# An LSTM and a conditioned adapter on one core: seeds of the first two steps in transfers of their own, the projection's weights on ScalarE's queue, five more zero matmuls

## The reference

```python
B, T, D = 16, 256, 256;  H = 256;  RANK = 8
xz = einsum('ntd,dk->ntk', x, Wx) + b              # the projection, 4 gates x 256
def step((h, c), xz_t):                            # 256 steps, one behind the other
    i, f, o, g = split(xz_t + h @ Wh)
    c = sigmoid(f) * c + sigmoid(i) * tanh(g)
    h = sigmoid(o) * tanh(c)
x = x + scan(step, (cond, 0), xz)

cn = layernorm(cond) * gamma + beta
a1, b1, a2, b2 = split(gelu(cn @ W1 + bias1) @ W2 + bias2)     # each (B, 256, 8)
mid = gelu(x @ base_down + (x @ a2) @ b2.T)
out = x + mid @ base_up.T + a1 @ (b1 . mid)
```

## Time and profile before

| | |
|---|---|
| median of 3 runs | 622.96 us (622.89, 622.96, 625.73) |
| the profiled execution | 622.3 us, span 620.3 us |
| granted TensorE clock, mean | 0.994 |
| TensorE busy | 600.6 us, 97% of the span |
| VectorE busy | 478.7 us, 77% |
| ScalarE busy | 386.7 us, 62% |
| GpSimd busy | 38.2 us, 6% |
| step 0's first matmul | 21.01 us into the span |
| step 1's first matmul | 25.18 us |

### The profile page before, as it was taken

One profiled execution on the slowest core, in us unless ns is written; L12 is line 12 of the kernel. 1 busy time (PEld: TensorE's weight loads), 2 busy tenths in 40 slices (PEclk: granted clock), 3 DMA queues, 4 the chain that ended last, 5 costly groups with the idle time before them and its releaser, 6 DMA issues.

```text
span 620.3 us, 34579 instructions
## 1 busy us (share of the span) xinstructions
PE 600.6 (97%) x14176; PEld 441.2 (71%) x14176; DVE 478.7 (77%) x2548; ACT 386.7 (62%) x2158; POOL 38.2 (6%) x78
## 2 busy tenths in 40 slices
PE   8789999999999999999999999999999999999997
PEld 5565555777777777777777777777777777777886
DVE  3566666888888888888888888888888888888773
ACT  2365555666666666666666666666666666666662
POOL 3000000000000000000000000000000000000000
PEclk9799999999999999999999999999999999999999
DMA  5893530232222113232321232322023232321201
GB/s 159 231 218 142 180 45 12 38 46 54 55 54 39 35 39 54 55 54 54 54 36 25 53 54 54 54 54 45 26 43 54 55 54 54 54 37 21 47 20 35
DMA packets 31471, 38.74 MB, mean 62 GB/s; under 512 B 3601, under 2 KB 29505, under 8 KB 30290
## 3 DMA queue, kind: packets, MB, share of 16 engines
q1 hardware_dynamic: 31282, 36.51, 27.4%
q0 software_dynamic: 32, 0.03, 0.0%
HBM read 15.55 MB, written 4.19 MB: 32 GB/s over the span
## 4 chain that ended last, share of the span: by engine, by line
PE 85%; DVE 7%; POOL 4%; issue 2%; DMA 1%; SPq 0%; POOLq 0%; ACT 0%; DVEq 0%; ACTq 0%
PE z L674 32%; PE x_bank L496 17%; PE aux L522 8%; PE z_o L674 7%; PE out_bank L545 5%; PE out_bank L603 4%; POOL xp L934 4%; PE aux L507 3%; PE aux L474 2%; PE out_bank L553 2%; PE aux L529 2%; DVE z L821 2%; DVE prod L831 1%; DVE gates L836 1%; DVE h_t L843 1%
## 5 line engine op out<-in xcount | busy, mean ns | idle before, releaser
L674 PEld LDWEIGHTS z<-wh,h_t 128*16 128x16 f32 x8160 | 155.1, 96 | 119.6 <-DVE h_t L843 96.0
L674 PE MATMUL z<-wh,h_t 128*16 128x96 f32 x8160 | 228.1, 248 | 5.6 <-DVE h_t L843 2.3
L821 DVE STREAM_TRANSPOSE z<-z 128x96 f32<-128x96 f32 x512 | 151.5, 298 | 87.2 <-PE z L674 60.3
L412 ACT ACTIVATE gates<-z 128x48 f32<-128x48 f32 x512 | 107.7, 210 | 141.9 <-DVE z L821 114.3
L496 PE MATMUL x_bank<-wx,x_t 128*128 128x256 f32 x512 | 156.2, 393 | 0.5 <-ACT x_t L330 0.5
L336 ACT ACTIVATE z<-seed 128x96 f32<-128x96 f32 x512 | 123.7, 242 | 5.6 <-DMA seed<-proj 5.6
L674 PE MATMUL z_o<-wh,h_t 128*16 128x64 f32 x4080 | 105.7, 219 | 0.4
L831 DVE SCALAR_TENSOR_TENSOR prod<-gates 128x32 f32<-128x32 f32 x512 | 97.8, 191 | 0.6
L836 DVE SCALAR_TENSOR_TENSOR gates<-prod 128x16 f32<-128x16 f32 x512 | 84.3, 165 | 8.7
L496 PEld LDWEIGHTS x_bank<-wx,x_t 128*128 128x128 f32 x512 | 80.7, 195 | 6.4 <-issue 1.5
L674 PEld LDWEIGHTS z_o<-wh,h_t 128*16 128x16 f32 x4080 | 80.6, 97 | 1.2 <-issue 0.9
(11 more groups left out here) (109 smaller groups left out, 445.9 us busy)
## 6 DMA issues: line engine op xcount, KB each, us to landing
seed<-proj SPq DMA_DIRECT2D x128, 128.0 KB, 4.0
w<-in_L_cond_W SPq DMA_DIRECT2D x4, 2048.0 KB, 9.9
x_nat<-in_x SPq DMA_DIRECT2D x32, 128.0 KB, 4.0
out<-y_nat SPq DMA_DIRECT2D x32, 128.0 KB, 3.7
wx<-in_L_cond_Wx SPq DMA_DIRECT2D x2, 512.0 KB, 5.6
wh<-in_L_cond_Wh SPq DMA_DIRECT2D x2, 256.0 KB, 6.5
wh<-in_L_cond_Wh SPq DMA_DIRECT2D x1, 512.0 KB, 6.2
w<-in_L_cond_W SPq DMA_DIRECT2D x1, 256.0 KB, 4.3
```

The source lines that it names most:

```text
L412: act.activation(gates[s % 2][m][:, 0:3 * B].rearrange("p (g b) -> p g b", b=B), zt[m].rearrange("p (g c) -> p g c", c=C)[:, :, 0:B], ACT. ...
L674: ins = pe.matmul(dst, h_prev[:, kc, :], rhs, start=False, stop=(kc == 1), skip_group_check=True)
L821: dve.transpose(zt[m], z_bank[m][:, 0:GC]).then_inc(turned[m], 1)
```

## The change

- A new tile `first_seed` holds the seeds of steps 0 and 1 (FIRST = 2). It is filled by eight transfers of 16 KB, four a step: SyncE issues those of quadrants 0 and 1, ScalarE those of quadrants 2 and 3, each in the order step 0, step 1, after the last quarter is in `proj`. Each step has its own semaphore. GpSimd clears `first_seed` ahead of the two `seed` tiles.
- The four full transfers of block 0 stay, with all eight steps in them, and are issued by SyncE behind its four small ones. ScalarE waits for them at the end of step 0 instead of ahead of it; steps 0 and 1 read `first_seed`, steps from 2 on `seed`.
- ScalarE issues the two transfers of Wx as its first instructions, ahead of its table load. SyncE's next loads move up by two.
- On ScalarE the doubling of Wh's g columns comes ahead of the copy of x of block 1 instead of behind it.
- TensorE runs five zero matmuls (128x96, into a projection bank) between the bias products and the projection.

```diff
+WARM_TILES = 5
+FIRST = 2
...
+        first_seed = sb("first_seed", [P, FIRST, ZW])
...
+        first_loaded = [sem(f"first_loaded{t}") for t in range(FIRST)]
...
+        def load_first_seeds(engine, quadrants):
+
+            engine.wait_ge(seeds_zeroed, 1)
+            engine.wait_ge(xz_ready, XQ)
+            for t in range(FIRST):
+                for j in quadrants:
+                    engine.dma_start(first_seed[32 * j:32 * j + B, t, :], proj[0][t:P:TB, ZW * j:ZW * (j + 1)])\
+                          .then_inc(first_loaded[t], 16)
...
     @block.sync: load_seed
-                    sp.wait_ge(seeds_zeroed, f.k + 1)
+                    sp.wait_ge(seeds_zeroed, f.k + 2)
...
-            load_cols(wx, Wx, 0, 0, 2 * H, "wx_if")
-            load_cols(wx, Wx, 2 * H, 2 * H, 2 * H, "wx_og")
...
+            load_first_seeds(sp, (0, 1))
             load_seed(Blk(0, 0))
             load_x(Blk(0, 0, 2))
...
     @block.scalar
+            load_cols(act, wx, Wx, 0, 0, 2 * H, "wx_if")
+            load_cols(act, wx, Wx, 2 * H, 2 * H, 2 * H, "wx_og")
             act.wait_ge(zeroed, 1)
...
-            evacuate_x(Blk(0, 1))
             act.wait_ge(w_loaded["wh"], 48)
             double_g(wh, 2 * H, wh_ready)
+            evacuate_x(Blk(0, 1))
+            load_first_seeds(act, (2, 3))
             act.wait_ge(bits_set, 1)
-            act.wait_ge(seed_loaded[0], 16 * NQ)
+            act.wait_ge(first_loaded[0], 16 * NQ)
             for m in both:
-                seed_bank(0, 0, m)
-            seed_o(0, 0)
+                seed_bank(first_seed, 0, m)
+            seed_o(first_seed, 0)
+            act.wait_ge(first_loaded[1], 16 * NQ)
...
+                    source = seed[ahead.par] if ahead.at_least(1) or s_next >= FIRST else first_seed
...
+                    if s == FIRST - 2 and not k.at_least(1):
+                        act.wait_ge(seed_loaded[0], 16 * NQ)
...
     @block.tensor
+            for i in range(WARM_TILES):
+                pe.matmul(x_bank[0][:, 0:GC], zeros[:, :], zeros[:, 0:GC], start=True, stop=True)
             project(Blk(0, 0), range(N_PIECES))
...
     @block.gpsimd
+            pool.memset(first_seed[:, :, :], 0.0).then_inc(seeds_zeroed, 1)
```

More of the change, by code:

```diff
@@ L231, in lstm_adapter, with load_cols @@
         last, last_early = follower(end), early(end)
+        def load_first_seeds(engine, quadrants):
[5 more added lines that the diff above has]
+                          .then_inc(first_loaded[t], 16)
+        by_half = "(m p) n -> p m n"
+        def load_cols(engine, dst, src, lo, src_lo, n, name):
+            engine.dma_start(dst[:, :, lo:lo + n], src.rearrange(by_half, m=NM)[:, :, src_lo:src_lo + n])\
+                  .then_inc(w_loaded[name], 16)
         @block.sync
@@ L258, in store_y @@
                   .then_inc(stored[a.lane][a.seq.par], 16)
[L260 to L264, removed]
             w2_q = W2.rearrange("(k p) (q n) -> q p k n", p=P, q=4)
@@ L272, in _ @@
             sp.dma_start(b_row[:, :], b.rearrange("(a n) -> a n", a=1)).then_inc(w_loaded["b"], 16)
-            load_cols(wx, Wx, 0, 0, 2 * H, "wx_if")
-            load_cols(wx, Wx, 2 * H, 2 * H, 2 * H, "wx_og")
             sp.dma_start(c_in[:, :], cond).then_inc(w_loaded["cond"], 16)
-            load_cols(wh, Wh, 2 * H, 3 * H, H, "wh")
-            load_cols(wh, Wh, 0, 0, 2 * H, "wh")
-            load_cols(wh, Wh, 3 * H, 2 * H, H, "wh")
+            load_cols(sp, wh, Wh, 2 * H, 3 * H, H, "wh")
+            load_cols(sp, wh, Wh, 0, 0, 2 * H, "wh")
+            load_cols(sp, wh, Wh, 3 * H, 2 * H, H, "wh")
             load_x(Blk(0, 1))
@@ L286, in _ @@
                          allow_slow_non_contiguous=True).then_inc(w_loaded["w1"], 16)
-            load_cols(up_raw, base_up, 0, 0, D, "up")
+            load_cols(sp, up_raw, base_up, 0, 0, D, "up")
             load_w2(QUARTERS[0])
             load_seed(Blk(0, 1))
-            load_cols(down_raw, base_down, 0, 0, D, "down")
+            load_cols(sp, down_raw, base_down, 0, 0, D, "down")
             def one_block(k, front):
@@ L332, in evacuate_x, with seed_bank, seed_o @@
                                scale=2.0).then_inc(xt_ready, 1)
-            def seed_bank(buf, s, m):
-                act.activation(z_bank[m][:, 0:GC], seed[buf][:, s, GC * m:GC * (m + 1)], ACT.Copy)\
+            def seed_bank(src, s, m):
+                act.activation(z_bank[m][:, 0:GC], src[:, s, GC * m:GC * (m + 1)], ACT.Copy)\
                    .then_inc(seeded[m], 1)
-            def seed_o(buf, s):
-                act.activation(o_bank[:, 0:OC], seed[buf][:, s, NM * GC:ZW], ACT.Copy).then_inc(seeded_o, 1)
+            def seed_o(src, s):
+                act.activation(o_bank[:, 0:OC], src[:, s, NM * GC:ZW], ACT.Copy).then_inc(seeded_o, 1)
             def gelu_mid(a):
@@ L432, in one_block @@
                         act.wait_ge(gates_ready[0], n)
-                        seed_bank(ahead.par, s_next, 0)
+                        seed_bank(source, s_next, 0)
                     tanh_cell(1)
@@ L436, in one_block @@
                         act.wait_ge(gates_ready[1], n)
-                        seed_bank(ahead.par, s_next, 1)
+                        seed_bank(source, s_next, 1)
                         act.wait_ge(gate_o_ready, n)
                         act.wait_ge(ht_ready[1], n + 1)
-                        seed_o(ahead.par, s_next)
+                        seed_o(source, s_next)
+                    if s == FIRST - 2 and not k.at_least(1):
+                        act.wait_ge(seed_loaded[0], 16 * NQ)
                     if s == TB - 2 and (front or k.p == 0):
```

## The result

The changed kernel is slower: 632.08 us (four runs, 630.24 to 633.47) against 623.2, a ratio of 1.0127 with a 95% interval of 1.0093 to 1.0161. Run again later beside other kernels it gave 1.0115 (1.0094 to 1.0137). The forecast was 625.0, range 621.3 to 627.4. That is 7 to 9 us more. The profiled execution, the fastest of the four, took 630.24 us with a span of 628.2, 7.9 more than before.

The account below looks back on a forecast made before the run. TensorE, busy 97% of the span, runs 256 dependent steps, so early delays persist: zero matmuls 1.08, x of block 0 0.3, x of block 2 0.1, clock 0.6 sum to 2.1 us on 622.96, giving 625.0, range 621.3 to 627.4.

Parts of the forecast that it names:

- the zero matmuls hide behind nothing: TensorE between bias products and projection: no gap there, five zero matmuls take 2.13 us, net cost 1.08 us.
- Wx's move gains nothing and delays x of block 0: Wx's transfers on ScalarE's queue: the projection did not wait for them; net cost 0.3 us through x of block 0.
- the 3 us that the first seeds gain: Between first seed issue and step 0: small transfers start step 0 4.0 us after the issue instead of 6.95.
- One sign that the prediction itself had set: Start of the bias products on TensorE: the prediction called itself wrong if they start later than 4.9 us.
- x of block 0 (0.6 us charged, bounds 0 to 1.5): Load that starts the chain: Wx's transfers running beside it delay it by 0.6 us, between 0 and 1.5.
- What comes back from the clock (half of both): Projection of block 0: clock rises at the same 11.8 us, returning 1.05 of 2.13 and half of 0.6 us.
- Step 0 at T + 4.0: Step 0's start on TensorE: 4.0 us after first seed issue, instead of 6.95, with small transfers landing in 2.5.
- T: SyncE's first seed issue after the last addition into proj: at 14.06 us before, forecast at 15.5 after.
- x of block 2 at T + 8.8: Load behind small and full seeds in SyncE's order: lands 8.8 us after first seed issue, costing 0.1 us.
- The clock in step 1 (0.6): Step 1's matmuls on TensorE: 2.2 us at the lower clock level in place of 0.3, losing 0.6 us more.
- From step 2 on nothing is changed and nothing has slack: All steps from step 2 to the end: the delay reached by then stays as it is, adding 0 us.
- The rival of the late clock: Projection of block 0: the clock's rise misses it, taking 6.83 us against 5.66; total 627.6 us, chance 0.17.

## Why the prediction was wrong

The direction and the places were right: the zero matmuls hide behind nothing, Wx's move gains nothing and delays x of block 0, the 3 us that the first seeds gain are spent in front of x of block 2, the clock is down for what follows. The sizes were not, and 2.1 us became 7 to 9. One sign that the prediction itself had set came true: the bias products started at 6.10, later than 4.9. In the profiled executions the 7.9 us are the forecast 2.1, 1.4 for x of block 0, 0.2 for the zero matmuls, 0.8 that did not come back from the clock, 1.1 for x of block 2, 0.1 for step 1 and 2.2 for everything from step 2 on.

**x of block 0 (0.6 us charged, bounds 0 to 1.5): 2.0 us.** Of the terms that were priced, this one is the furthest off. It landed at 5.37, 5.30, 5.21, 5.41, 5.82 and 6.38 with Wx on ScalarE's queue, and at 3.34 to 3.44 in every kernel with Wx on SyncE. The row of the 16 KB transfer that took 5.8 us among the weights was the nearest one, and I did not let it set the upper bound. Wx's first half, issued in the same instant with four times the bytes, was the first to land, at 5.07; its packets were the first to move. Its issue was the shorter one, 0.44 us against 0.69; that this put it ahead is likely and not shown. The Trainium skill ("DMA: Bandwidth & Descriptors", Issuing engines are not separate DMA queues) says that such transfers interleave. From 3.65 on they do here, 81 packets of ScalarE's queue beside 104 of SyncE's; before that they did not, and this cost x three quarters of its delay. The prediction named the rule and gave the small transfer that starts the chain too little for it.

**What comes back from the clock (half of both): less.** I took it that the rise stays at 11.8 us. It came near 15.2 in the changed kernel, where the projection's records change from 0.427 to 0.216 us apart, so of 2.0 + 2.38 only 0.58 came back and not 1.35. The assumption failed for Wx's part, where the rise moved along in all six profiles. It also varies by itself: in the six kernels that are alike up to the projection (before and the five others with Wx on SyncE and no zero matmuls) the projection took from 5.13 to 6.72 us. One profile could not fix this term to better than 1.6 us.

**Step 0 at T + 4.0: T + 3.3.** The 16 KB transfers landed 1.8 us after issue, not 2.5:

```profile
first_seed<-proj SPq DMA_DIRECT2D x1, 16.0 KB, 1.8
...
x_nat<-in_x SPq DMA_DIRECT2D x1, 128.0 KB, 4.8
```

Nothing hung on it.

**x of block 2 at T + 8.8: T + 9.9** (9.3 to 10.3 over the runs). Half a microsecond is the issue: 0.64 for a small transfer with its pause, where I had taken 0.51 from the row of cond, though I had the seed's 0.64 as the other end. The rest is the transfer itself, 4.8 us to landing against 4.2. With it the part of x of block 2 is 1.2 us instead of 0.1.

**The clock in step 1 (0.6): 0.7** (5.0 later at step 1's first matmul, 5.7 at the end of step 2). Right.

**"From step 2 on nothing is changed and nothing has slack": 2.2 us.** This is the largest part of the miss, and the prediction had it at nothing. The sentence is true of the instructions, but not of what they meet. The loads of W2 fall on other steps, TensorE's waits without a semaphore come behind other steps, and one of them had 3.4 us at the lower clock level behind it. That such a wait goes with W2's second part is shown (the run in which it moved), and so is the fixed place in the program. Of the 2.2 us, 1.7 are placed by step 16: 0.5 is more waiting and some 1.2 falls into steps 12 and 13 with the lower level. The last 0.5 comes and goes in pieces of 0.2 to 0.4 us between steps 45 and 237, and what makes them stays open.

The rival of the late clock came nearest. The rise did come late and T did move by 3.8 us. It had the zero matmuls' full price and up to 1.5 for x of block 0 in it, but it also made the projection 1.2 us longer, and the projection became 0.6 shorter; its terms behind T had the forecast's sizes. A sum of the prediction's own upper bounds (1.2 for the projection, 2.13 for the zero matmuls, 1.5 for x, 0.7 for the issues, 0.1 and 0.6 behind them) is 6.2 us, where the range stopped at +4.4. Even that is under the 7 to 9 measured, since nothing in it stands for x beyond 1.5 or for what happens from step 2 on.

## What to carry to other kernels

A second issuing queue can let a large load go ahead of a small one that was issued in the same instant: before putting a large load on it, look which small one is first in the chain, and let that land alone. When a wait is shortened, price the next item in the same queue as well, with every issue that now stands ahead of it; here one line, the load of x of block 2 moved ahead, was what made the early seeds worth having (ratio 1.002 without it, 0.9972 with it). Filler matmuls put where TensorE had no gap cost 2.2 to 2.4 us and brought no earlier rise of the clock, and the rise is no constant of the kernel.

## What the runs showed of the hardware

- On SyncE an issue of a seed transfer takes 0.57 to 0.63 us whether it moves 16 or 128 KB; on ScalarE a small one takes 0.56 to 0.75. Issues of x took 0.54 to 0.69 us in most places, and 0.8 to 1.8 in others.
- Four 128 KB transfers from SBUF to SBUF in rows of 1 KB land about 1.1 us apart, some 120 GB/s, with the DMA share above 1; loads from HBM in the same execution reach over 400 GB/s. The length of the rows alone is not the reason: x of block 0, also 128 KB in rows of 1 KB but from HBM, was moved from 2.2 to 3.05 us, in less than 0.9 us.
- TensorE can stand still for 0.6 to 2.6 us with no semaphore to wait for. In all 22 cases a 2 MB load was under way, and the wait stood behind one of four counts of matmul records, the same in every kernel up to one record.
- The clock column prints 1.00 before its first event. The distance between records is what tells the level there.
